# Message passing on one NeuronCore: the one-hots of three layers made on VectorE in place of ScalarE

## The reference

```
for l in range(3):
    agg = segment_sum(h[src], dst, num_segments=n)   # 200,000 gathered rows of 128 floats
    z = (1.0 + eps[l]) * h + agg
    hid = maximum(z @ W1[l] + b1[l], 0.0)
    h = hid @ W2[l] + b2[l]
x = layernorm(x + h)
# attention layer: e = leaky_relu([h[src], h[dst]] @ w) @ a; softmax over edges of one src;
# out = segment_sum(h[src] * att, dst);  x = layernorm(x + out)
```

## Time and profile before

| what | value |
| --- | --- |
| timed runs | 9,327.69 us median (9,326.17 to 9,331.99) |
| profiled execution | span 10,761.6 us; no other timer of it is given |
| granted TensorE clock, mean | 0.672 |
| three layers, gathers only | 77.6 to 2,346.5, 2,412.1 to 4,680.6, 4,730.7 to 7,001.4 us |
| score stage, gathers | 7,132.5 to 9,574.9 us |
| weighted stage and final norm | 9,623 to 10,761.6 us |
| HBM traffic | 876 MB, 81 GB/s over the span |

### The profile page before, as it was taken

One profiled execution on the slowest core, in us unless ns is written; L12 is line 12 of the kernel. 1 busy time (PEld: TensorE's weight loads), 2 busy tenths in 40 slices (PEclk: granted clock), 3 DMA queues, 4 the chain that ended last, 5 costly groups with the idle time before them and its releaser, 6 DMA issues.

```text
span 10761.6 us, 137184 instructions
## 1 busy us (share of the span) xinstructions
PE 4749.1 (44%) x27323; PEld 4216.7 (39%) x27324; DVE 3994.5 (37%) x13681; ACT 3909.3 (36%) x11178; POOL 6943.5 (65%) x7392
## 2 busy tenths in 40 slices
PE   3323222343322323342333332256666666667776
PEld 2222222232222222232222222256666666666665
DVE  2222222222222222222222222256556655568888
ACT  3333333333333333333333333322222222237777
POOL 5666666656666666656666666646666666658886
PEclk6555555566555555565555555677778777789998
DMA  3111111122111111121111111145555555544444
GB/s 81 45 46 45 45 46 45 46 59 51 45 45 46 45 46 46 45 65 47 46 45 46 45 46 45 46 139 149 146 147 148 148 147 147 146 132 138 138 139 133
DMA packets 918236, 875.96 MB, mean 81 GB/s; under 512 B 253109, under 2 KB 764001, under 8 KB 918175
## 3 DMA queue, kind: packets, MB, share of 16 engines
q0 software_dynamic: 239728, 516.96, 18.5%
q1 hardware_dynamic: 614765, 259.14, 8.7%
q10 hardware_dynamic: 63698, 99.36, 3.3%
HBM read 734.15 MB, written 137.96 MB: 81 GB/s over the span
## 4 chain that ended last, share of the span: by engine, by line
issue 26%; another core or an unknown queue 23%; DVE 20%; DVEq 17%; PE 11%; ACT 2%; DMA 0%; ACTq 0%; POOL 0%; SPq 0%; POOLq 0%
DVE agg L1585 8%; DVEq L1562 7%; DVEq L468 5%; DVE agg L1571 4%; PE psum L1251 4%; PE psum L1276 2%; DVEq L1580 2%; PE psum L1270 2%; DVE big L1818 2%; DVEq L1593 1%; DVE work L1692 1%; DVE work L1699 1%; PE psum L1178 1%; DVE work L1689 1%
## 5 line engine op out<-in xcount | busy, mean ns | idle before, releaser
L1178 PE MATMUL psum<-work,rows 128*128 128x128 f32 (+1 forms) x9408 | 2056.2, 394 | 4728.1 <-DVE agg L1585 2465.2
L766 POOL DMA_INDIRECT rows<-table_g,idx_now x3136 | 2966.9, 946 | 1688.0 <-issue 1061.4
L1178 PEld LDWEIGHTS psum<-work,rows 128*128 128x128 f32 x9408 | 1825.5, 284 | 4959.6 <-issue 2822.9
L1585 DVE TENSOR_TENSOR agg<-agg,psum 128x128 f32 x4704 | 1351.4, 287 | 5323.6 <-remote 3145.3
L933 ACT ACTIVATE work<-big,one_col 128x512 f32<-128x512 f32 x1176 | 817.9, 710 | 3315.9 <-remote 2837.2
L766 POOL DMA_INDIRECT rows<-in_x,idx_now x1568 | 1483.3, 946 | 799.3 <-issue 467.6
L923 ACT ACTIVATE big<-iota_w,rel_now 128x128 f32<-128x128 f32 (+1 forms) x4704 | 1501.6, 396 | 429.5 <-remote 345.0
L766 POOL DMA_INDIRECT rows<-table_p,idx_now x784 | 764.3, 975 | 480.8 <-SPq L599 254.9
L1010 ACT ACTIVATE work<-psum 128x256 f32<-128x256 f32 x784 | 295.2, 387 | 1864.9 <-remote 1129.9
L1251 PE MATMUL psum<-work 128*128 128x98 f32 x3168 | 624.3, 362 | 689.0 <-DVE work L1692 362.4
L1251 PEld LDWEIGHTS psum<-work 128*128 128x128 f32 x3168 | 569.5, 269 | 741.3 <-DVE work L1692 392.9
(11 more groups left out here) (211 smaller groups left out, 5718.4 us busy)
## 6 DMA issues: line engine op xcount, KB each, us to landing
rows<-x_of SPq DMA_DIRECT2D x415, 256.0 KB
rows<-table_g,idx_now POOLq DMA_INDIRECT x3136
work<-rel_rows ACTq DMA_DIRECT2D x196, 256.0 KB
x_of<-rows SPq DMA_DIRECT2D x196, 256.0 KB
big<-lo_rows ACTq DMA_DIRECT2D x208, 192.0 KB
x_of<-work SPq DMA_DIRECT2D x147, 256.0 KB
rows<-in_x,idx_now POOLq DMA_INDIRECT x1568
idx_now<-src_t SPq DMA_DIRECT2D x784, 4.0 KB
```

Source lines behind the costliest of these rows:

```text
L766: pool.indirect_dma_start(out=to, out_offset=None, in_=table, in_offset=bass.IndirectOffsetOnAxis(ap=idx_now[:, at:at + 1], axis=0)) \
L1178: ins = pe.matmul(sums_at(q, t % QUAD)[:, 0:wide], ring[:, t, :], span_hot[q][:, t % QUAD, 0:wide], start=True, stop=True)
L1585: dve.tensor_tensor(to, to, sums_at(q, j)[:, 0:P], ALU.add).then_inc(added[j], 1)
```

## The change

- ScalarE's function `one_hots` goes, with its two steps and L941. ScalarE then has nothing to do in the sums of a layer.
- VectorE makes each tile's one-hot by one instruction, `tensor_scalar(iota == rel)`, whose scalar operand is the column of `rel_t` at a register address. The one-hots of quad q+2 are made after quad q-1 was added and before quad q is waited for.
- The addresses in `agg` are prepared: all window numbers are multiplied by 128 once (`scale_windows`, before the layers and once more before the weighted stage) and loaded multiplied.
- The sums of a quad lie in one PSUM bank (`ps[q]`) instead of two; the 256-wide sums of a turn's first tile lie in `ps[4]`.
- All waits of a quad compare with one value: `quads_summed` replaces `rows_used` in the layers and counts quads, and `added`, `seconds_added` and `hot_ready` start at values that make the same number fit. The second window's addition comes before the first.

```diff
+        def load_sums_at(first, n=HALF):
+            _, values = nc.values_load_multi_w_load_instructions(
+                sums_at_win[0:1, ds(first, n)], engines=(DVE_E,), min_val=0, max_val=(WINS - 1) * D,
+                skip_runtime_bounds_check_because="D times a tile's window, by its making")
+            return list(values)
-        def sums_at(q, j):
-            return ps[2 * q + j // 2][:, (j % 2) * 2 * P:(j % 2 + 1) * 2 * P]
+        def sums_at(q, j, wide=P):
+            if q == 0 and j == 0:
+                return ps[IN_HAND][:, 0:wide]
+            return ps[q][:, j * P:j * P + wide]
...
 (GpSimd, gather_lane)
-                            pool.wait_ge(rows_used, USED - RING + no * T2 + lap * LAP + lane * HALF + j + QUAD)
+                            pool.wait_ge(quads_summed, no * QUADS2 + lap * (LAP // QUAD) + (lane * HALF + j) // QUAD + 1)
...
 (ScalarE)
-            def one_hots(l):
...
-                        ins = act.activation(span_away[q % 2][:, j, 0:wide], iota_w[:, 0:wide], ACT.Abs, bias=rel_now[:, t:t + 1])
...
-                    act.activation(span_hot[q][:, :, 0:P], span_away[q % 2][:, :, 0:P], ACT.Relu, bias=one_col[:, :],
-                                   scale=-1.0).then_inc(hot_ready, 1)
...
 (TensorE, sum_rows)
-                            pe.wait_ge(added[QUAD - 1], quad + 1)
-                            pe.wait_ge(hot_ready, quad + 3)
+                            pe.wait_ge(added[QUAD - 1], Q_USED + quad + 2 - IN_HAND)
+                            pe.wait_ge(hot_ready, Q_USED + quad + 2 - IN_HAND)
...
 (VectorE)
+            def scale_windows():
+                own.add(dve.tensor_single_scalar(sums_at_win, tile_win, D.bit_length() - 1, ALU.logical_shift_left))
+                own.wait()
...
+            def one_hots(q, first):
+                for j in range(QUAD):
+                    wide = 2 * P if q == 0 and j == 0 else P
+                    ins = dve.tensor_scalar(span_hot[q][:, j, 0:wide], iota_w[:, 0:wide], rel_t[:, ds(first + j, 1)], None, ALU.is_equal)
+                ins.then_inc(hot_ready, 1)
+            def add_quad(q, value, sums_to, second_to):
+                dve.wait_ge(quads_summed, value)
+                if q == 0:
+                    dve.tensor_tensor(second_to, second_to, sums_at(0, 0, 2 * P)[:, P:2 * P], ALU.add).then_inc(seconds_added, IN_HAND)
+                    dve.wait_ge(seconds_added, value + IN_HAND - 1)
+                for j in range(QUAD):
+                    to = sums_to[(q % 2) * QUAD + j]
+                    if j:
+                        dve.wait_ge(added[j - 1], value)
+                    dve.tensor_tensor(to, to, sums_at(q, j), ALU.add).then_inc(added[j], 1)
+            def sum_turn(l, turn, hots_from):
+                values = [Q_USED + l * QUADS2 + turn * IN_HAND + q + 1 for q in range(IN_HAND)]
...
+                    for q in range(2 * h, 2 * h + 2):
+                        dve.wait_ge(added[QUAD - 1], values[q])
+                        if q < hots_from:
+                            one_hots((q + 2) % IN_HAND, turn * TPI + (q + 2) * QUAD)
+                        add_quad(q, values[q], sums_to, sums_to[-1])
             def layer_sums(l):
-                with dve.Fori(0, TURNS2) as i:
...
+                dve.wait_ge(g_taken, 2 * QUADS)
+                for q in range(2):
+                    one_hots(q, q * QUAD)
+                with dve.Fori(0, TURNS2 - 1) as i:
+                    sum_turn(l, i, IN_HAND)
+                sum_turn(l, TURNS2 - 1, 2)
```

More of the change, by code:

```diff
@@ L208, in gnn @@
         assert QUAD * ROW + QROWS <= 2 * T2
[L209 to L212, removed]
+        sums_at_win = big[0:1, CHUNKS * PW - QROWS:CHUNKS * PW].bitcast(i32)
+        assert max(6 * QROWS, rest_at + HI + P) <= CHUNKS * PW - QROWS
         e_src = rows[:, 0:QROWS].bitcast(i32).rearrange("p (r e) -> p r e", r=RG)
@@ L912, in deviation @@
                 act.activation(std[:, s, 0:n], mean_var[:, s, 0:n, 1], ACT.Sqrt, bias=ln_eps[:, :]).then_inc(std_ready, 1)
-            def one_hots(l):
[L916 to L922, removed]
-                        ins = act.activation(span_away[q % 2][:, j, 0:wide], iota_w[:, 0:wide], ACT.Abs, bias=rel_now[:, t:t + 1])
[L924 to L932, removed]
-                    act.activation(span_hot[q][:, :, 0:P], span_away[q % 2][:, :, 0:P], ACT.Relu, bias=one_col[:, :],
-                                   scale=-1.0).then_inc(hot_ready, 1)
[L936 to L942, removed]
-                    for q in range(IN_HAND):
-                        distances(i, q)
-                        if q >= 1:
-                            hots(i, q - 1)
-                    hots(i, IN_HAND - 1)
-            act.sem_inc(hot_ready, 2)
-            act.wait_ge(g_taken, 2 * QUADS)
-            one_hots(0)
             for b in range(BLOCKS):
@@ L1335, in _ @@
             for j in range(QUAD):
-                dve.sem_inc(added[j], IN_HAND)
+                dve.sem_inc(added[j], Q_USED + (j == QUAD - 1))
+            dve.sem_inc(seconds_added, Q_USED)
+            dve.sem_inc(hot_ready, Q_USED + 1 - IN_HAND)
             dve.sem_inc(score_ready, 2)
@@ L1591, in layer_sums @@
-            def layer_sums(l):
-                with dve.Fori(0, TURNS2) as i:
-                    for h in range(2):
-                        windows = load_windows(i * TPI + h * HALF, DVE_E)
-                        second = load_windows(i + REAL, DVE_E, 1) if h == 0 else None
-                        for q in range(2 * h, 2 * h + 2):
-                            add_quad(l, i, q, windows, second)
+                    wide = 2 * P if q == 0 and j == 0 else P
+                    ins = dve.tensor_scalar(span_hot[q][:, j, 0:wide], iota_w[:, 0:wide], rel_t[:, ds(first + j, 1)], None, ALU.is_equal)
@@ new lines, in sum_turn @@
+            def sum_turn(l, turn, hots_from):
+                values = [Q_USED + l * QUADS2 + turn * IN_HAND + q + 1 for q in range(IN_HAND)]
+                for value in values:
+                    dve.compute_val(value)
+                for h in range(2):
+                    windows = load_sums_at(turn * TPI + h * HALF)
+                    second = load_sums_at(turn + REAL, 1) if h == 0 else []
+                    sums_to = [sums_of(window) for window in windows + second]
+                    for q in range(2 * h, 2 * h + 2):
[3 more added lines that the diff above has]
+                        add_quad(q, values[q], sums_to, sums_to[-1])
@@ L1774, in _ @@
             own.wait()
+            scale_windows()
             dve.tensor_copy(hi_t, hi_t.bitcast(i32)).then_inc(hi_ready, 1)
@@ L1822, in weights_of @@
                 dve.lower_ap(given)
-                windows = load_windows(added_next * HALF, DVE_E) if added_next is not None else None
+                windows = load_sums_at(added_next * HALF) if added_next is not None else None
                 dve.wait_ge(hot_act, len(HOT_ACT) * (group + 1))
```

50 lines of the change are left out of this document (16 added, 34 removed).

## The result

| | median us | lowest to highest | runs |
| --- | --- | --- | --- |
| before | 9,326.93 | 9,324.65 to 9,331.99 | 4 |
| changed | 9,601.57 | 9,600.28 to 9,606.49 | 4 |

The ratio is 1.0295 with a 95% interval of 1.028 to 1.031: 275 us slower, where the prediction said 23 and its range ended at 9,465.

A forecast was written before the change was run, and what follows sets the result against it. Timed runs were taken as the sum of GpSimd's gathers plus what lies between them. 9,327.7 + 21 (comparisons against gathers) + 1 (layer start) + 1 (scale_windows) = 9,351 us, 0.25% slower; range 9,300 to 9,465.

The forecast's parts named there:

- What bounds the layers: In the layers, GpSimd's gathers set the time, 1.25 us from start to start, with no room to wait in timed runs.
- The pace of register instructions: VectorE's slow register instructions in a layer, 0.69 us each, were held to belong to the recorded execution, not timed runs.
- 38 us above: The recorded span without GpSimd's 1,396 us of waiting, 9,366 us, lay 38 us above the timed runs.
- ScalarE's work goes, VectorE's turn grows, one bank and one value: In the layers' turns, these were worth nothing: VectorE needs 16.3 us at worst beside 20.0 us of gathers.
- Layer starts and scale_windows, 1 us each: 1 us for the second layer's start behind the comparisons, 1 us for the second scaling between score and weighted stage.
- The comparisons against the gathers, 21 us: In the layers, VectorE's comparisons stretch gathers: 60 ns per 512 columns, scaled by (1/4)^2 to 3.8 ns per 128; 21 us.
- Rival A: In the layers, the comparisons miss the gathers: 9,330 us, chance 0.26.
- rival B: In the layers, a comparison holds gathers for its whole instruction: 172 us (9,502), or 105 us (9,435); chance 0.18.
- one multiplication less inside, of the same count; nothing: In the weighted stage, the address instructions lose one multiplication but keep their count: no effect on the time.
- Rival C: In the timed layers, GpSimd still waits for multiplied quads and the change removes it: 38 us faster, 9,290; chance 0.10.
- Rival D: VectorE becomes the bound in the layers if a comparison costs over 0.77 us: 9,710 at 0.85 us; chance 0.03.
- if the time moves while the gathers' mean does not: The sign given for a wrong forecast: kernel time changes but the mean gather duration doesn't.

The follow-up runs named there:

- e4: The kernel before with its window-number table at a multiple of 64 bytes, nothing else changed: 9,328.66 us, ratio to before 1.0001.
- e9: The changed kernel with only the weighted stage loading unscaled window numbers from the old place, without the second scaling: 9,359.17 us, 1.0029 of before.
- e1: The changed kernel with its scaled window-number table begun 6 words earlier, at a multiple of 16 bytes: 9,358.27 us, 1.0033 of before.
- e7: e1 with the numbers 0 to 255 that the layers' comparisons read held in PSUM instead of SBUF: 9,338.04 us, 1.0007 of before.
- e3: The kernel before with its window-number table begun 6 words later, at byte 8 of 16, nothing else changed: 9,583.87 us, 1.0274 of before.
- e13: e7 with one wait instead of two for the fetched factors in each half-turn of the weighted stage: 9,326.83 us, 1.0 of before.
- e12: The kernel before with one wait instead of two for the fetched factors in each half-turn of the weighted stage: 9,320.51 us, 0.9993 of before.
- e2: The changed kernel with its scaled window-number table at a multiple of 64 bytes: 9,355.44 us, 1.0029 of before.
- e8: The changed kernel with its scaled window-number table at byte 4 of 16, one word behind e1's place: 9,605.41 us, one run.
- e11: e7 with one load of sixteen window numbers per turn of the weighted stage instead of two of eight: 9,340.23 us, 1.0009 of before.
- e10: The kernel before with one load of sixteen window numbers per turn of the weighted stage instead of two of eight: 9,344.76 us, 1.0014.

## Why the prediction was wrong

*What bounds the layers*: right. The gathers follow each other every 1.25 us in both kernels.

*The pace of register instructions*: the conclusion that timed runs don't have it was right and its reason wrong. Recording doesn't slow them (see the result). Only a part of the register instructions was slow in that trace, and none in its weighted stage. The "38 us above" dissolve as well: in e4 the span is 9,326.5 and the timed median 9,328.7.

*ScalarE's work goes, VectorE's turn grows, one bank and one value*: right, all hidden; the turn swallows even loads of 1.8 us (e9).

*Layer starts and scale_windows, 1 us each*: right in size. The pauses between the stages grew by 1.5, 1.2 and 1.7 us and one shrank by 1.4; 3 us more lie behind the last gather, which the sum didn't have.

*The comparisons against the gathers, 21 us*: right in mechanism, once the layers run at the pace of the forecast; the size is in part luck. e1 has 20.7 us more in its layers than e4, and e7 takes them away by changing nothing but where the comparison reads. Rival A (the comparisons miss the gathers) and rival B (172 or 105 us) are out. But the 60 ns for a comparison of 512 columns came from the disturbed trace. In e4 the same two groups of gathers lie 11 and 9 ns over their medians (968 and 966 against 957), which makes 13.9 us in place of 23.5 and, by the same scaling, some 12 us for the layers. So the input was too large and the scaling by (1/4)^2 too small, and the two nearly cancelled. The changed kernel itself shows only 12.8 us: beside its slow loads fewer comparisons met a gather, 197 gathers over 960 ns against e1's 325. Its 99th percentile is 1,015 ns, 71 over the median, and e1's is 1,031, 87 over it, near the 64 ns for which by the prediction's estimate 128 columns stream. The Trainium skill's page "SBUF — State Buffer", section "SBUF: two separate sides", lets a VectorE operation in a two-port mode hold the shared ports for its whole instruction. That something holds the gathers beside such comparisons agrees with e1, and that it is gone with a source in PSUM is shown by e7; the whole instruction as its length does not agree: the comparisons take 0.30 us on average, and the stretches end at 0.13 us but for four of the 325.

*The weighted stage, "one multiplication less inside, of the same count; nothing"*: this is the step that failed. It counted the instructions behind the load and took the load itself for unchanged. Of the 275 us, 261 are here: some 254 by the slow loads, as e3 shows without any of the change, and the remaining 7 by the gap described under e13, which e1 and e7 keep and whose cause is open. The load's count, its width and its place in the order were the same; its source was another tile at another offset, and the step never asked where the eight words lie. And the load lies on a chain that nothing covers: in the layers 588 equally slow loads cost nothing (e9), here 208 cost about 1.25 us each. The offset follows from the code, although no row of before showed that it matters; that the weighted stage runs through the load could have been read from a chain through L468 to L1829 in it, which the prediction didn't read since the change seemed to leave that stage alone.

*Rival C* (a wait in the timed layers) did not happen. *Rival D* named the right engine, but VectorE became no bound in the layers. In the weighted stage its sequencer paced the kernel already before the change (e12), and the slow loads made that path longer while its busy time there stayed.

*What would make the prediction wrong*: "if the time moves while the gathers' mean does not". The mean moved by 2.7 ns (13 us) and the time by 275.

## What to carry to other kernels

When a change moves the data of an instruction, price the instruction again, even if its count and shape stay: a table that registers are loaded from belongs at a multiple of 16 bytes, and a few words of padding were worth 243 us here. Look at every stage that uses an edited helper, and ask in each whether something covers that line. Where an engine issues its DMAs beside VectorE's work from SBUF to SBUF, a source in PSUM can be the better one though the instruction gets slower, as long as VectorE isn't the bound.

## What the runs showed of the hardware

- Register loads: one word 0.30 us at any of the places tried; eight words 0.60 us at a multiple of 16 bytes and 1.85 us at 4 or 8 bytes past one (VectorE); on TensorE, as medians, 0.59 and, at 8 bytes past one, 2.40 us; sixteen words 1.1 us at a multiple of 16.
- These fit a load that fetches 16 bytes at a time where it can (1, 2 and 4 fetches of some 0.3 us) and word by word where it can't (8 of 0.23 us, on TensorE 8 of 0.30). That is a reading of the numbers; no run looked inside. The Trainium skill's page "Runtime: NRT & Kernel Launch", section "Instruction fetch mechanics", gives about 200 ns per register, and describes such loads as coming from HBM. The loads here come from SBUF: the placed ones take 75 ns per register, the misplaced ones 231 ns. No run loads registers from HBM.
- Fp32 comparisons of 128 columns (of 256 for one tile in sixteen) held up GpSimd's gathers by 20 us over 4,704 of them if they read SBUF, and not measurably if they read PSUM; reading PSUM cost those of 128 columns 42 ns each on average.
- In the changed kernel, in e1, e2, e7, e8, e9, e11, e13 and in e10, VectorE's sequencer has one gap of about 0.15 us in place of 0.03 to 0.05 in each turn of the weighted stage, at a place that differs between the kernels. The kernel before, e3, e4 and e12 have none there. Beside e4, the stage is 7 to 12 us longer where the loads are quick.
